# Macaron block on one core: queries and keys of the attention turned by DMA crossbar transfers, SBUF to SBUF

## The reference, cut to what matters

```python
x = x + 0.5 * ffn(layernorm(x))          # x: 8 sequences x 256 tokens x 128
q, k, v = (layernorm(x) @ W.T).reshape(B, L, 16, 8)   # 16 heads of 8
q, k = rope(q), rope(k)
scores = einsum('blhd,bshd->bhls', q, k) / sqrt(8)
x = x + einsum('bhls,bshd->blhd', softmax(scores), v).reshape(B, L, 128) @ W_o.T
x = x + 0.5 * ffn(layernorm(x))
```

## Time and profile before

| | |
|---|---|
| median of 3 runs | 355.51 us (354.25 to 356.33) |
| the profiled execution | span 351.5 us from its first to its last instruction; the page gives no other time for it |
| TensorE busy | 83% of the span, granted clock 0.944 in the mean |
| VectorE, ScalarE, GpSimd busy | 67%, 57%, 46% |
| the attention | about 104 to 268 us of the span |

### The profile page before, as it was taken

How to read it: one execution, slowest core, us unless ns; L and a number is a source line. 1 busy time by engine, 2 the same in 40 slices (tenths; PEclk the granted TensorE clock), 3 DMA queues, 4 the chain that set the end, 5 groups by cost and what they waited for, 6 DMA issues and landing times.

```text
span 351.5 us, 6586 instructions
## 1 busy us (share of the span) xinstructions
PE 292.5 (83%) x2124; PEld 185.0 (53%) x2146; DVE 233.9 (67%) x634; ACT 198.8 (57%) x441; POOL 161.5 (46%) x295
## 2 busy tenths in 40 slices
PE   0679948999964779999999999998999895999950
PEld 0564626666634245555655555555475463666630
DVE  6986332344654789898989898997966647344332
ACT  1125211554445469899898989897858421454520
POOL 5736730365877325352535264541210674166560
PEclk9999986999995599999999999999999999999995
DMA  6992135012113000000000000000000012511135
GB/s 192 176 351 80 53 98 107 24 40 67 40 37 91 0 0 4 0 3 2 0 2 3 2 1 2 2 1 3 2 2 1 30 55 75 136 47 37 47 101 184
DMA packets 21584, 18.41 MB, mean 52 GB/s; under 512 B 5072, under 2 KB 19152, under 8 KB 21296
## 3 DMA queue, kind: packets, MB, share of 16 engines
q1 hardware_dynamic: 19056, 12.87, 14.3%
q0 software_dynamic: 2496, 5.13, 4.6%
HBM read 10.29 MB, written 7.71 MB: 51 GB/s over the span
## 4 chain that ended last, share of the span: by engine, by line
PE 31%; DVE 27%; POOL 14%; issue 14%; ACT 4%; another core or an unknown queue 3%; DMA 3%; SPq 1%; POOLq 0%; DVEq 0%; ACTq 0%
PE bank L1014 24%; POOL y_by_token L342 11%; DVE negmax L842 11%; PE bank L1196 4%; DVE qT L835 3%; DVE xn L650 2%; PE bank L1023 1%; DMA x<-in_x 1%; DVE sh L756 1%; ACT kT L579 1%; DVE rs L859 1%; DMA y_by_token<-ys,xg 1%; DVE onehotb L692 1%; DVE stats L660 1%
## 5 line engine op out<-in xcount | busy, mean ns | idle before, releaser
L842 DVE TENSOR_REDUCE negmax<-bank 128x2 f32<-128x512 f32 x128 | 84.0, 683 | 9.1 <-PE bank L1014 6.2
L572 ACT ACTIVATE probs<-bank 128x512 f32<-128x512 f32 x128 | 72.1, 603 | 15.9 <-PE bank L1014 15.4
L342 POOL DMA_INDIRECT y_by_token<-ys,xg x46 | 44.9, 976 | 52.2 <-issue 26.5
L1014 PE MATMUL bank<-qT,kT 128*128 128x256 bf16 x256 | 49.2, 275 | 1.2 <-ACT qT L588 0.3
L1014 PE MATMUL bank<-rgu,xgT 128*128 x92 | 47.2, 596 | 0.6 <-ACT xgT L542 0.6
L333 POOL DMA_INDIRECT xs_sorted<-xs,slot x32 | 31.9, 998 | 33.6 <-ACT xs L502 17.2
L1014 PE MATMUL bank<-kT,qT 128*128 128x512 bf16 x106 | 42.6, 407 | 5.3 <-ACT kT L579 2.6
L806 DVE TENSOR_TENSOR rh<-rsg,bank 128x256 f32<-128x256 f32 x46 | 19.3, 419 | 41.2 <-ACT rsg L550 40.7
L550 ACT ACTIVATE rsg<-bank 128x256 f32<-128x256 f32 x46 | 17.6, 383 | 37.3 <-PE bank L1014 37.3
L1196 PE MATMUL bank<-tabb,parts 128*128 128x128 bf16 x384 | 31.3, 229 | 5.9 <-POOL parts L376 2.3
L1196 PEld LDWEIGHTS bank<-tabb,parts 128*128 128x128 bf16 x384 | 26.1, 103 | 16.5 <-POOL parts L376 7.9
(11 more groups left out here) (114 smaller groups left out, 497.9 us busy)
## 6 DMA issues: line engine op xcount, KB each, us to landing
rgu<-in_rgu SPq DMA_DIRECT2D x1, 2048.0 KB
xg<-xs_sorted SPq DMA_DIRECT2D x6, 258.0 KB, 4.5
xs_sorted<-xg SPq DMA_DIRECT2D x1, 1483.5 KB, 15.8
xg<-xs_sorted SPq DMA_DIRECT2D x6, 193.5 KB, 3.8
x<-in_x SPq DMA_DIRECT2D x4, 256.0 KB, 4.9
rdn<-in_rdn SPq DMA_DIRECT2D x1, 1024.0 KB
xs<-y_by_token SPq DMA_DIRECT2D x8, 128.0 KB, 3.0
xs<-y_by_token SPq DMA_DIRECT2D x4, 256.0 KB, 4.1
```

The lines of the kernel that those rows point to most:

```text
L342: g.indirect_dma_start(y_dram, bass.IndirectOffsetOnAxis(ap=xg[:, j, D:ROW].bitcast(U32), axis=0), ys[:, j, :], None, bounds_check=N + SLO ...
L572: a.activation(probs[:, h % 8, :], stbank[st_bank(i, h)][:], ACT.Exp, scale=float(DH) ** -0.5).then_inc(exp_done, 1)
L842: v_.tensor_reduce(negmax[:, w, t, h0 + 2 * pair:h0 + 2 * pair + 2], sbank[k % 2][:].rearrange("p (a s) -> p a s", a=2), AX.X, ALU.max, ne ...
L1014: return t_.matmul(o_, l, r, start=start, stop=stop, **k)
```

## The change

The PE transposes "qa", "ka", "qb" and "kb", ScalarE's copies of keys and VectorE's copies of these queries are gone. The parts of q and of k are two tensors now. `kparts` has four slots of 64 columns for a pair of heads: even head, zeros, zeros, odd head. Turned as two blocks of 128 columns, a pair gives both planes of kT with their zero halves. SP issues all turning as DMA transposes from SBUF to SBUF (`turn_rows`), in the order batch, half, row tile: 4 pairs of keys (128 partitions x 1024 columns, 256 KB) and 4 pairs of queries (128 x 512, 128 KB) each time, 32 DMAs of keys and 32 of queries in all. They wait for `part3` of the row tile, and from batch 2 on for the transposed scores that read qT and kT of batch b-2 last. They are issued behind the loads of the first ffn. The plain scores wait for the half's four DMAs (`qk_turned`). "ma" and "mb" stay on TensorE. ScalarE takes the copies of oT (step 10) and, in turns 0 and later, of xT (step 14) from VectorE. ScalarE writes the second parts in steps 8 and 9, not 11 and 12, and GpSimd writes the third parts before `split_max` in turns 0 and later. GpSimd's remainder is two instructions for a row tile, not one.

```diff
+        qparts = [sb(f"qparts{u}", [P, 2, H, KROWS], BF16) for u in range(2)]
+        kparts = [sb(f"kparts{u}", [P, 2, H // 2, 4, KROWS], BF16) for u in range(2)]
...
-        uses = ["qa", "ka", "qkv0", "qkv1", "back", "mb", "qb", "kb", "oT", "wo", "ma", "xT"]
+        uses = ["qkv0", "qkv1", "back", "mb", "oT", "wo", "ma", "xT"]
...
+            def turn_rows(b, half, t):
+                u, s = b % 2, slice(t * P, (t + 1) * P)
+                pairs, heads = slice(half * HH // 2, (half + 1) * HH // 2), slice(half * HH, (half + 1) * HH)
+                sp.wait_ge(part3, 2 * b + t + 1)
+                if b >= 2:
+                    sp.wait_ge(st_filled, H * (b - 2) + HH * (half + 1))
+                sp.dma_start_transpose(
+                    kT[u][:, pairs, :, s].rearrange("p r a s -> p (r a) s"),
+                    kparts[u][:, t, pairs].rearrange("p r q c -> p (r q c)")).then_inc(qk_turned[half][u], 16)
+                sp.dma_start_transpose(
+                    qT[u][:, pairs, s], qparts[u][:, t, heads, :].rearrange("p h c -> p (h c)")).then_inc(qk_turned[half][u], 16)
...
+                if n == 0:
+                    attention_rows()
...
-                    g.tensor_tensor(r3(rem), r3(rot), flat[:, :, 2 * DH:3 * DH], ALU.subtract).then_inc(rem_ready, 1)
+                    for q in range(2):
+                        cols = slice(q * D, (q + 1) * D)
+                        ins = g.tensor_tensor(by_pair(rem[:, t, cols]), by_pair(rot[:, t, cols]), part_at(u, t, q, slice(2 * DH, 3 * DH)), ALU.subtract)
+                    ins.then_inc(rem_ready, 1)
...
-                if i == -1:
+                if T.pr:
                     third(0)
+                if T.pr and i != -1:
+                    third(1)
                 if T.m:
                     split_max(i + 1, 0)
-                if T.pr and i != -1:
-                    third(0)
-                if T.pr:
+                if i == -1:
                     third(1)
...
-                    if n == 1 and T.m:
-                        copy_keys(0, 0)
-                    if n == 3 and T.m:
-                        copy_keys(0, 1)
...
-                    if n == (7 if i == -1 else 9) and T.m:
-                        copy_keys(1, 0)
-                        copy_keys(1, 1)
-                    if n == (8 if i == -1 else 11) and T.pr:
+                    if n == 8 and T.pr:
                         second(0)
-                    if n == (8 if i == -1 else 12) and T.pr:
+                    if n == (8 if i == -1 else 9) and T.pr:
                         second(1)
+                    if n == 10 and T.f:
+                        act.wait_ge(filled["oT"], i)
+                        a.copy(oT[:], work[uses.index("oT") % 2][:, 0:L]).then_inc(emptied["oT"], 1)
...
+                    if n == 14 and T.nx and i >= 0:
+                        act.wait_ge(filled["xT"], i + 4)
+                        a.copy(xnT2[:, v, :], work[uses.index("xT") % 2][:, 0:L]).then_inc(emptied["xT"], 1)
...
                     if k == 0:
-                        for name in (("qa", "ka"), ("qb", "kb"))[half]:
-                            pe.wait_ge(emptied[name], b + 1)
+                        pe.wait_ge(qk_turned[half][w], 64 * (b // 2 + 1))
...
-                    if n == 0 and T.m:
-                        pe.wait_ge(part3, 2 * (i + 1) + 2)
-                        turn_parts("qa")
-                    if n == 1 and T.m:
-                        pe.wait_ge(part3, 2 * (i + 1) + 2)
-                        turn_parts("ka")
...
-                    if n == (5 if i == -1 else 7) and T.m:
-                        turn_parts("qb")
-                    if n == (5 if i == -1 else 8) and T.m:
-                        turn_parts("kb")
```

More of the change, by code:

```diff
@@ L146, in build @@
         rem = sb("rem", [P, 2, 2 * D], F32)
-        parts = [sb(f"parts{u}", [P, 2, 2, H, KROWS], BF16) for u in range(2)]
+        qparts = [sb(f"qparts{u}", [P, 2, H, KROWS], BF16) for u in range(2)]
+        kparts = [sb(f"kparts{u}", [P, 2, H // 2, 4, KROWS], BF16) for u in range(2)]
         qT = [sb(f"qT{u}", [P, H // 2, L], BF16) for u in range(2)]
@@ L203, in build @@
         s_filled, s_reduced, m_split = sem("s_filled"), sem("s_reduced"), sem("m_split")
+        qk_turned = [sems(f"qk_turned{half}", 2) for half in range(2)]
         st_filled, exp_done, pv_done, pv_copied = sem("st_filled"), sem("exp_done"), sem("pv_done"), sem("pv_copied")
@@ L224, in build, with part_at, by_pair @@
         AHEAD = 4
+        def part_at(u, t, q, rows):
+            if q:
+                return kparts[u][:, t, :, 0:4:3, rows]
+            return qparts[u][:, t, :, rows].rearrange("p (r a) c -> p r a c", a=2)
+        def by_pair(a_):
+            return a_.rearrange("p (r a d) -> p r a d", a=2, d=DH)
         class Turn:
@@ L263, in _, with attention_rows @@
         def _(sp):
+            def turn_rows(b, half, t):
[9 more added lines that the diff above has]
+                    qT[u][:, pairs, s], qparts[u][:, t, heads, :].rearrange("p h c -> p (h c)")).then_inc(qk_turned[half][u], 16)
+            def attention_rows():
+                for b in range(B):
+                    for half in range(2):
+                        for t in range(2):
+                            turn_rows(b, half, t)
             xv = x_in.rearrange("p (c i d) -> c p i d", i=CHUNK, d=D)
@@ L348, in _ @@
             for u in range(2):
[L349 removed]
+                g.memset(kparts[u][:].bitcast(F32), 0.0).then_inc(consts_set, 1)
             for c in range(CHUNKS):
@@ L361, in _ @@
                     g.memset(v5[:, :, s_, :, 16 + s_:17 + s_], 1.0).then_inc(consts_set, 1)
-                g.memset(parts[u][:, :, 1, :, MCOL:MCOL + 3], 1.0).then_inc(consts_set, 1)
+                for t in range(2):
+                    g.memset(part_at(u, t, 1, slice(MCOL, MCOL + 3)), 1.0).then_inc(consts_set, 1)
             def turn(T, piece=None):
@@ L371, in split_max @@
                     m = negmax[:, w, :, h0:h0 + HH]
-                    mc = [parts[w][:, :, 0, h0:h0 + HH, MCOL + k] for k in range(3)]
+                    mc = [qparts[w][:, :, h0:h0 + HH, MCOL + k] for k in range(3)]
                     st.link(g.tensor_copy(mc[0], m))
@@ L381, in clear_max_parts @@
                         pool.wait_ge(filled["mb"], i + 1)
-                    g.memset(parts[u][:, :, 0, :, MCOL:MCOL + 3], 0.0)
+                    g.memset(qparts[u][:, :, :, MCOL:MCOL + 3], 0.0)
                 def rotate(t):
@@ L572, in exponentials @@
                     a.activation(probs[:, h % 8, :], stbank[st_bank(i, h)][:], ACT.Exp, scale=float(DH) ** -0.5).then_inc(exp_done, 1)
-                def copy_keys(half, k):
-                    name = ("ka", "kb")[half]
-                    act.wait_ge(filled[name], i + 2)
-                    src = work[uses.index(name) % 2][:].bitcast(BF16).rearrange("p (r s) -> p r s", r=4)
-                    ins = a.copy(kT[v][64 * k:64 * k + 64, 4 * half:4 * half + 4, k, :], src[64 * k:64 * k + 64])
-                    if k:
-                        ins.then_inc(emptied[name], 1)
                 def copy_queries(name):
@@ L597, in part @@
                     for q in range(2):
-                        part_of = src[:, t, q * D:(q + 1) * D].rearrange("p (h d) -> p h d", h=H)
-                        dst = parts[u][:, t, q, :, 0:MCOL].rearrange("p h (s d) -> p h s d", s=6)[:, :, into[q], :]
-                        ins = a.copy(dst, part_of.unsqueeze(2).to_broadcast([P, H, rows, DH]))
+                        part_of = by_pair(src[:, t, q * D:(q + 1) * D])
+                        dst = part_at(u, t, q, slice(0, MCOL)).rearrange("p r a (s d) -> p r a s d", s=6)[:, :, :, into[q], :]
+                        ins = a.copy(dst, part_of.unsqueeze(3).to_broadcast([P, H // 2, 2, rows, DH]))
                     ins.then_inc(done, 1)
@@ L966, in turn @@
                         copy_queries("mb")
-                    if n == 7 and T.m:
-                        copy_queries("qb")
-                    if n == 10 and T.f:
-                        dve.wait_ge(filled["oT"], i)
-                        v_.tensor_copy(oT[:], work[uses.index("oT") % 2][:, 0:L]).then_inc(emptied["oT"], 1)
                     if n == (6 if i == -1 else 10) and T.nx:
@@ L975, in turn @@
                         add_attention()
-                    if n == (11 if i == -1 else 14) and T.nx:
+                    if n == 11 and i == -1:
                         copy_turned()
@@ L1195, in turn_parts @@
                             at = (2 * pair + t) * P
-                            ins = t_.transpose(to[:, at:at + P], parts[w][:, t, q, h:h + 2, :].rearrange("p a c -> p (a c)"), identb)
+                            ins = t_.transpose(to[:, at:at + P], qparts[w][:, t, h:h + 2, :].rearrange("p a c -> p (a c)"), identb)
                     ins.then_inc(filled[name], 1)
```

20 lines of the change are left out of this document (5 added, 15 removed).

## The result

The changed kernel takes 344.87 us (median of 4 runs, 343.62 to 346.59) against 354.88 us of the kernel before, run beside it: a ratio of 0.973, interval 0.969 to 0.977. It is faster by 10.0 us. The other 1.7 us of the 10.0 are no part of the two traces: the span of before lies 3.4 us under its median, the span after 1.7 under its own.

What follows compares the result with a forecast made beforehand. TensorE, VectorE and ScalarE were taken as nearly full (17.5, 16.7, 16.5 of about 18.4 us a turn), all needing relief. Span 351.5 - 14.7 + 2.0 = 338.8 us, plus 4.0 to the median: 343 us, range 334 to 430.

Steps and rivals of the forecast that it cites:

- The turns: Attention turns 0 to 6: 2.1 us saved each, a little under VectorE's 2.2 us release; 14.7 us in all.
- 3.7 x 32/48 = 2.5 us of TensorE: Attention turn: removing 32 of a batch's 48 PE transposes, busy 3.7 us together, frees 2.5 us of TensorE.
- The chain's 2.5 us: Attention turn's chain of waits: would lose three query copies (0.69, 0.60, 0.60 us) and 0.57 us of TensorE's queue.
- T = 13.2: SP's queue: time T for a batch's transfers, 12 x 1.1 us per 128 KB; bounds 5.2 and 33 us.
- The margin of 1 us: Attention turns: a half's transfers need 8.5 us of about 9.4 available before step 4, so they hide.
- Moved at no cost: GpSimd in the turns: splitting the remainder adds at most 0.41 us a row tile, covered; earlier third parts delay nothing.
- The first batch: Start of attention: uncovered transfers delay the first product 3.2 us, less 1.4 for query copies gone: +2, between 0 and +6.
- ScalarE's copy of 128x256 at 0.5: Attention turns: each copy of oT or xT moved to ScalarE taken as 0.5 us, between 0.42 and 0.606.
- Rival 1: Attention: if T exceeds the turn, scores wait on SP's queue; 215.3 + 8T, deciding from T = 17.5; chance 0.43.
- Rival 2: Attention turns: with T near 16.4, transfers fit the turn but not the margin; gain lost, about 355.5; chance 0.07.
- Rival 3: Attention turns: VectorE's chain of maxima alone sets the pace, gaining little over 0.57 us a turn; some 353; chance 0.05.
- the estimate of 63 us: SP's queue: the skill's 1309 ns per 128x128 block, applied one after another to a batch's 48 blocks; not used in the sum.

Runs made afterwards that it cites:

- experiment 3: Changed kernel with 32 PE transposes of each batch put back on TensorE beside the transfers; 338.22 us, ratio 0.992 to the kernel before.
- experiment 6: Changed kernel with two more 128x1024 VectorE copies a turn and the copies of oT and xT back on VectorE; 335.51 us, ratio 0.981 to the kernel before.
- experiment 7: Changed kernel with three 64x1024 ScalarE copies put back in each turn with a batch to turn; 337.22 us, ratio 0.986 to the kernel before.
- experiment 8: Changed kernel with each transfer cut in two, sixteen a batch, the same bytes; 375.21 us, ratio 1.099 to the kernel before.
- experiment 4: Changed kernel with second parts in steps 11 and 12 and third parts behind the split of the maxima, as before; 332.09 us, ratio 0.971 to the kernel before.
- experiment 1: Changed kernel with the last turn's copy of oT back on VectorE; 328.36 us, ratio 0.963 to the kernel before.
- slower group: The last four of the twelve follow-up runs, beside which the kernel before took 355.3 us; the two main traces are like it.
- faster group: The first eight of the twelve follow-up runs, beside which the kernel before took 341.5 us.
- experiment 10: Kernel of experiment 1 with GpSimd's clears of vx and qparts moved behind the first scatters; 344.11 us, ratio 0.969 to the kernel before.
- experiment 11: Kernel of experiment 1 with both row tiles in one transfer, four a batch, buffers laid out by head pairs; 345.26 us, ratio 0.972 to the kernel before.
- experiment 12: Kernel of experiment 1 with both the later clears and the four transfers a batch; 344.70 us, ratio 0.973 to the kernel before.
- experiment 2: Changed kernel with two more 128x1024 clears, so that GpSimd clears as much as before; 332.18 us, ratio 0.975 to the kernel before.

## Why the prediction was right

Forecast 343, measured 344.9. The sign held, and so did the mechanism: the transfers hide behind the turns, and relieving three nearly full engines shortens each turn. The sum was less exact than the 1.9 us say. In spans the forecast was 338.8 and the trace has 343.2, a gain of 8.3 us and not of 12.7. What brought the time closer was the step from the span to the median, taken as 4.0 us from the kernel before; the changed kernel's is 1.7. These 2.3 us are luck. The two terms that were missing (-2.3 and +3.2) nearly cancel and helped nothing.

- **The turns: -14.7 predicted, -9.5 measured** (seven turns, 1.36 us each in the mean instead of 2.1; 0.9 to 1.4 in the first six, 2.2 in the last). This is the term that was mis-sized. VectorE and ScalarE came down as given. TensorE came down by 1.4 instead of 2.5 us. The step "3.7 x 32/48 = 2.5 us of TensorE" took a group's busy time for what it keeps from others. TensorE's timeline of before, in the turn of the earlier trace rows, shows what it keeps:

```profile
189.06 0.61 PE L1196 MATMUL bank<-tabb,parts 128*128 128x128 bf16 x8
189.50 0.38 PE L1014 MATMUL bank<-qT,kT 128*128 128x256 bf16 x2
...
189.94 0.61 PE L1196 MATMUL bank<-tabb,parts 128*128 128x128 bf16 x8
190.38 0.38 PE L1014 MATMUL bank<-qT,kT 128*128 128x256 bf16 x2
```

  Eight transposes are busy for 0.61 us, but the next product starts 0.44 us behind their start. Four groups less are 4 x 0.44 = 1.8 us. The smallest release was then TensorE's and not VectorE's, and "a little under the smallest" would have been some 1.4. That is near the 1.36 of the mean; the turn shown gave 1.15. Experiments 3, 6 and 7 say why not all of the release arrives: the engines hand over to one another, and none of the three has to be full to cost time.
- **The chain's 2.5 us** (three query copies and 0.57 of queue) was no measure of the gain, and was read too high. The copy at 188.22 is that of "mb", which follows the transposes at 186.62 and stays. The 0.57 of "issue" is not TensorE's queue: it lies on VectorE, between its maximum, which starts at 180.76 and takes 0.69 us, and its copy at 181.37. The forecast took 2.1 from the releases and not from here, so this cost it nothing.
- **T = 13.2 predicted, 10.6 measured**, within the bounds of 5.2 and 33. The value was near, and the reason for it wrong. It is not 1.1 us for each 128 KB: 256 KB and 128 KB take nearly the same, 1.25 and 1.28 us, and experiment 8 shows half the bytes at the full price. Had the change issued sixteen transfers, my price by bytes would have missed the loss of a tenth.
- **The margin of 1 us** was enough: the half took 7.1 us in the first batch and not 8.5, and the queue rests 6.6 us in a turn. In experiment 4, with the late order, it is used up, and TensorE waits for transfers in five turns, without a loss in the time. "Moved at no cost" held.
- **The first batch: +2.0 predicted, +0.3 measured** up to "ma". The +2.0 were +3.2 at the first product less 1.4 for copies that are gone. The first product came 1.8 us later against SP's last load, since the half took 7.1 us and not 8.5, and 1.5 came back behind it.
- **Two terms were missing**: -2.3 us for the clears that shrank, and +3.2 us behind the last turn, of which experiment 1 gives back 2.7. "The instructions before and after it are the same" stands ahead of the prediction, and it isn't so for the clears: the diff changes the size of a buffer, and its clear is as long as the buffer. And I counted the copy of oT that was moved to ScalarE at 0.5 us in the full loop (it takes 0.40), but did not ask what is queued behind it in the turn that has no loop any more.
- **ScalarE's copy of 128x256 at 0.5** measured 0.38 to 0.40.
- **The rivals.** Rival 1 did not come about, as T stayed under 17.5. It was the right one to fear: experiment 8 is this kernel with T = 20.8. Rival 2 needed T = 16.4. Rival 3's mechanism, that the maxima alone set the pace, fell with experiment 3, where VectorE had 2.6 us to spare in a turn of 17.9 and TensorE's added work lengthened it.
- **The rules of the Trainium skill.** SP's queue shows 1.25 us for an instruction of 8 blocks, about 2.6 us until 4 of them have landed, and 10.6 us for the 48 blocks of a batch. The figure of VectorE: DVE Perf Modes, section "The three transpose paths", 1309 ns for a block of 128x128, is near what one instruction costs here, whatever its blocks up to eight. Read as a price for each block it would have made the estimate of 63 us, and the trace speaks against that reading. Of the 350 to 400 GB/s of Advanced Engine Details and Errata, section "X-Bar Transpose (TRN2)", the queue shows 1.57 MB in 10.6 us, 148 GB/s: at these sizes the issue and not the bandwidth is the limit.

**Open.** What makes VectorE and ScalarE, and TensorE behind them, stand for some microseconds in the shared parts of both ffns, and why the length differs between kernels. It is seen in every kernel profiled in the slower group and in none of the faster, and its length is of the size of what experiments 10 to 12 should have won, but no run here takes it away alone. The queues that bring the program's instructions (q8 and q14) carry 0.38 MB in the changed kernel and as much in experiment 1, which does not stand still, so their bytes give no reason. Open too is what separates the two groups. So the gain of the best version measured, experiment 1 at 0.963, is confirmed in the faster group only.

## What to carry to other kernels

A transposing DMA between SBUF tiles cost its queue 1.25 us an instruction here, for 2 blocks as for 8, so put 8 blocks into each rather than 2 or 4, count instructions before bytes, and see whether a batch's worth fits its period: here 8 instructions for a batch made the kernel 2.7% faster and 16 made it 10% slower. Four of twice the size shortened the queue's time to 7.6 us and won nothing. Where several engines are nearly full, relieve them together, and take as an engine's release what the next instruction's start shows, not the busy time of the group. Of an instruction that is moved to another in-order engine, look at the last turn of the loop, where the next stage is queued behind it.

## What was unexpected of the hardware

- VectorE's small operations stand still while GpSimd clears memory: a cast of 128x32 takes 3.39 us beside clears of 128x2048 f32, 2.53 and (experiment 2, with more of them) 5.22 beside clears of 128x1024, and 0.18 without them. An engine's timeline shows this as a long instruction, not as a wait, so no view names the releaser. The cast outlasted more than one clear: in the kernel before it ran from 14.74 to 18.13, over the rest of one clear, the 1.80 us of the next and the third of 0.95, which ended at 18.09. The Trainium skill, SBUF — State Buffer, section "Who interferes with whom", has VectorE and GpSimd take turns at a shared pair of ports, with casts and `tensor_scalar` among the forms of VectorE that can want it and `tensor_reduce` not. By that rule, the trace agrees: these two forms were held, and in the changed kernel a `tensor_reduce` of 128x32 at 13.80, beside a clear that started at 13.79, took 0.19 us as it does elsewhere.
- The issue time of a transposing DMA was the same for 2 blocks (1.24 to 1.25 us), 4 (1.26 to 1.28) and 8 (1.23 to 1.33), a few longer ones aside; three plain loads of 256 KB took 1.38 us together on the same queue. In experiment 11, with 16 and 8 blocks in turn, it is 1.3 to 3.2 us. From issue to landing it is 2.4 to 2.6 us for 2 and 4 blocks, 3.3 for 8, and 4.4 and 4.0 in experiment 11.
- Around the end of 2.6 us of TensorE's idle time the granted clock was 0.66 over five microseconds, and over the five from 280.5, behind 3.7 us of it, 0.79. In the kernel before, where TensorE was idle for 2.45 us at 290 us, the clock stayed at 1.00. The runs here don't say what makes the difference.
- VectorE can stand for 3.6 to 8.0 us, and TensorE behind it for 2.5 to 5.9, in a wait that no instruction on the core ends. The same kernel is 4% faster in another group of runs whose traces show none of these waits at these places.
